# Four output stores of a layered cross network sent as nine row-strided transfers each, with a load moved ahead of them

## The chip, the cores and the metric

The kernel runs on one core of a Trainium2 chip. The metric is the device time of one execution in microseconds; before the change it is 1279.35 us as the median of three runs (1278.41 to 1281.69 us).

## The reference, cut to what matters

The input `x0` has 16384 rows of 4096 float32 numbers. Six layers follow one another, each with one weight vector `w_l` and one bias vector `b_l`:

```python
def step(x, wb):
    wi, bi = wb
    xw = jnp.matmul(x, wi)        # one number for each row
    x_new = x0 * xw + bi + x
    return (x_new, None)
x, _ = jax.lax.scan(step, inputs, (w, b))
```

Each row of the result is therefore that row of `x0` times one number, plus a vector that is the same for all rows. The kernel has to read 256 MiB and to write 256 MiB, and does little else to each number.

## The kernel before, in words

The rows are cut into 128 tiles of 128 rows. A tile is 128 partitions by 4096 float32, 2 MiB, and a row of it is 16 KB that lie together in memory. Ten tiles fit on the chip at once: `tiles` has 5 places for pairs (`N_SLOTS`), with 2 tiles in each (`TB`).

A tile goes through this: SyncE (SP) issues its load. VectorE (DVE) transposes it in two pieces into `blocks` (L261), TensorE (PE) multiplies these with the weights of all layers into `dots` (L405 in the loop over pairs, L363 for the first 2 and the last 24 tiles, which are done one by one), ScalarE (ACT) spreads the sums (L219), a few small steps on PE, ACT and DVE turn them into the one number of each row (`scale`), and DVE writes the result over the tile (L285, two halves of 2048 columns) and raises `tiles_done`. SP then issues the store.

All large transfers go through SP's queue, in an order that the code writes out by hand. In iteration `n` SP waits until tile `n` is done, issues its store (L155), then waits until tile `n - 3` has been stored (`LAG` is 3), since the tile to be loaded next goes to the same place, and issues the load of tile `n + 7` (L143). Each place has one semaphore for its landed loads (`x_landed`) and one for its stores (`y_stored`). A transfer raises its semaphore by 16 in all. A wait for a store is therefore a wait for all its shares, whichever of the chip's 16 DMA engines carries them. The last tile is stored in four parts by columns (L168), and the kernel ends when all stores have landed.

In the startup ScalarE issues six small loads through a queue of its own: the 24 strips of `w` (24 partitions of 4 KB), four loads of rows of `b` (6 partitions each, 2 rows of 2 KB on each), and the 24 strips of `b` (24 partitions of 4 KB).

Of the kernel before, what the change touches and what calls it, by code (L numbers as in the profile page):

```python
# [9 lines left out]
P = 128  # L10
Q = 32
G = P // Q
TB = 2
# [5 lines left out]
N_SLOTS = 5  # L19
HEAD, TAIL = 2, 24  # L20
STORE_PARTS = 4
LAG = 3
LAST_PAIR_OF_PREP = N_SLOTS - 1


def cross_network(nc, x, w, b, out):
    rows, D = x.shape
    L = w.shape[0]
    n_tiles = rows // P
# [13 lines left out]
    out_pairs = out.rearrange("(q t p) d -> q p t d", p=P, t=TB)  # L43
# [4 lines left out]
    with ExitStack() as ctx:  # L48
        def sb(name, shape):
            return ctx.enter_context(nc.sbuf_tensor(name, shape, F32))  # L50
# [4 lines left out]
        def sem(name):  # L55
            return ctx.enter_context(nc.semaphore(name))

        tiles = sb("tiles", [P, N_SLOTS, TB, D])
# [29 lines left out]
        y_stored = [[sem(f"y_stored{s}_{t}") for t in range(TB)] for s in range(N_SLOTS)]  # L88
# [41 lines left out]
        def place_of(n):  # L130
            return n // TB, n // TB % N_SLOTS, n % TB

        def weights_of(g):
            rows = slice(g * Q, (g + 1) * Q)
            into = weights[rows, :, g * LP:g * LP + L].rearrange("p (j k) l -> p j l k", j=G)
            turned_rows = w_turned[rows, :].rearrange("p (k q) -> p k q", q=Q)
            return into, turned_rows[:, :, 0:STRIPS].rearrange("p k (l j) -> p j l k", j=G)

        @block.sync
        def _(sp):  # L140
            def load(n):
                q, s, t = place_of(n)
                sp.dma_start(tiles[:, s, t, :], x_pairs[q, :, t, :]).then_inc(x_landed[s][t], 16)  # L143

            for n in range(TB * LAST_PAIR_OF_PREP):
                load(n)
            load(TB * LAST_PAIR_OF_PREP + 1)
            sp.wait_ge(weights_ready, G)
            sp.wait_ge(bias_summed, 2)
            sp.wait_ge(strips_summed, 1)  # L150
            load(TB * LAST_PAIR_OF_PREP)
            def store(n):
                q, s, t = place_of(n)
                sp.wait_ge(tiles_done, n + 1)
                sp.dma_start(out_pairs[q, :, t, :], tiles[:, s, t, :]).then_inc(y_stored[s][t], 16)  # L155

            for n in range(n_tiles - 1):
                store(n)
                into = n - LAG + TB * N_SLOTS
                if TB * N_SLOTS <= into < n_tiles:  # L160
                    q, s, t = place_of(into)
                    sp.wait_ge(y_stored[s][t], 16 * (q // N_SLOTS))
                    load(into)
            q, s, t = place_of(n_tiles - 1)
            for i in range(STORE_PARTS):
                at = slice(i * D // STORE_PARTS, (i + 1) * D // STORE_PARTS)
                sp.wait_ge(tiles_done, n_tiles + i)
                sp.dma_start(out_pairs[q, :, t, at], tiles[:, s, t, at]).then_inc(y_stored[s][t], 16)  # L168
            for n in range(n_tiles - TB * N_SLOTS, n_tiles):
                q, s, t = place_of(n)  # L170
                last_stores = 1 if n < n_tiles - 1 else STORE_PARTS
                sp.wait_ge(y_stored[s][t], 16 * (q // N_SLOTS + last_stores))

        @block.gpsimd
        def _(pool):
# [23 lines left out]
        def _(act):  # L199
# [7 lines left out]
            for g in range(G // 2, G):  # L207
                place = weights_of(g)
                nc.scalar.copy(place[0], place[1]).then_inc(weights_ready, 1)  # L209
# [31 lines left out]
        def _(dve):  # L241
# [53 lines left out]
            for g in range(G // 2):  # L295
                place = weights_of(g)
                nc.vector.tensor_copy(place[0], place[1]).then_inc(weights_ready, 1)
# [142 lines left out]
```

## Time and profile before

| | |
|---|---|
| median of three runs | 1279.35 us |
| the profiled execution, its own time | 1279.0 us |
| its span in the profile | 1277.3 us |
| VectorE busy | 91% of the span |
| DMA, queue of SP | 98.7% of 16 engines' span |
| TensorE busy | 62% |

The span is the time from the first to the last instruction of the profiled execution, and 1.7 us of that execution's own time lie around it. The share of a DMA queue is the time that its packets took, divided by 16 times the span: 98.7% means that nearly all of the 16 engines carried something nearly all the time. A packet is a row of a transfer, or the write of 4 bytes with which an engine tells a semaphore that its share has landed. The profile counts such writes among the packets under 512 B.

### The profile page before, as it was taken

To read this page: it belongs to the slowest core of one execution; us is meant where nothing else is said; L and a number is where in the kernel's file an instruction comes from. 1 tells how busy PE (TensorE), PEld (TensorE's weight loads), DVE (VectorE), ACT (ScalarE), POOL (GpSimd) and SP (SyncE) were. 2 spreads that over 40 slices of the span, in tenths; PEclk is the share of its full clock that TensorE was granted. 3 is DMA by queue.
4 is the path that set the end of the run, shared out by engine and by line. 5 is a ranking of instruction groups with operands and counts; after the bars stand their busy time and mean duration, and the time that the engine had idled before them with its cause. 6 is when DMAs were issued, how large, how long until landed. Compare 5 with 4: busy or idle time off the path is not lost.

```text
span 1277.3 us, 22775 instructions
## 1 busy us (share of the span) xinstructions
PE 790.4 (62%) x10394; PEld 739.8 (58%) x10394; DVE 1167.0 (91%) x652; ACT 109.5 (9%) x390; POOL 4.3 (0%) x17
## 2 busy tenths in 40 slices
PE   7677666666556556656566556565666457676661
PEld 3666656656456556556566556565565457675561
DVE  5999999998898988989989889899999999999893
ACT  2000000000000000000000000000000011111110
POOL 1000000000000000000000000000000000000000
PEclk9777787777877877877777787777777877778766
DMA  9999999999999999999999999999999999999994
GB/s 369 427 399 432 430 431 432 431 431 430 432 430 433 428 433 429 432 429 432 431 432 430 431 430 431 432 431 431 431 431 430 431 428 429 428 427 428 427 412 172
DMA packets 37480, 537.74 MB, mean 421 GB/s; under 512 B 4192, under 2 KB 4192, under 8 KB 4800
## 3 DMA queue, kind: packets, MB, share of 16 engines
q1 hardware_dynamic: 37296, 536.89, 98.7%
q8 instruction: 28, 0.46, 0.1%
q10 hardware_dynamic: 144, 0.30, 0.1%
q14 instruction: 12, 0.10, 0.0%
HBM read 268.73 MB, written 268.44 MB: 421 GB/s over the span
## 4 chain that ended last, share of the span: by engine, by line
DMA 58%; DVE 33%; issue 4%; PE 2%; SPq 1%; ACTq 0%; ACT 0%; DVEq 0%
DMA tiles<-in_r_inputs_dram 48%; DVE tiles L285 17%; DVE blocks L261 16%; DMA out_dram<-tiles 9%; DMA tiles<-in_L_rec_b_dram 1%; PE dots L363 1%; SPq L155 1%; DVE scale L273 0%; PE strips L353 0%; PE dots L405 0%; ACTq L202 0%; PE scratch L343 0%; ACT spread L219 0%; PE turned L374 0%; DVEq L48 0%
## 5 line engine op out<-in xcount | busy, mean ns | idle before, releaser
L405 PE MATMUL dots<-blocks,weights 128*64 128x128 f32 x6528 | 554.7, 349 | 308.6 <-DVE blocks L261 308.5
L405 PEld LDWEIGHTS dots<-blocks,weights 128*64 128x64 f32 x6528 | 526.6, 185 | 329.0 <-DVE blocks L261 328.8
L261 DVE STREAM_TRANSPOSE blocks<-tiles 128x2048 f32<-128x2048 f32 x256 | 576.1, 2288 | 76.5 <-issue 65.5
L285 DVE SCALAR_TENSOR_TENSOR tiles<-tiles,scale,c_low 128x2048 f32<-128x2048 f32 x129 | 299.1, 2319 | 0.9
L285 DVE SCALAR_TENSOR_TENSOR tiles<-tiles,scale,scratch 128x2048 f32<-128x2048 f32 x129 | 299.8, 2325 | 0.0
L363 PE MATMUL dots<-blocks,weights 128*64 128x64 f32 x3328 | 148.8, 273 | 52.4 <-DVE blocks L261 45.3
L363 PEld LDWEIGHTS dots<-blocks,weights 128*64 128x64 f32 x3328 | 144.9, 187 | 56.6 <-issue 56.4
L219 ACT ACTIVATE spread<-dots,group_mask 128x128 f32<-128x128 f32 (+1 forms) x308 | 82.3, 350 | 1038.8 <-PE dots L405 849.9
L374 PE MATMUL turned<-layer_sel,spread 128*128 128x8 f32 x512 | 71.0, 262 | 93.1 <-ACT spread L219 93.1
L374 PEld LDWEIGHTS turned<-layer_sel,spread 128*128 128x128 f32 x512 | 64.3, 194 | 109.3 <-issue 80.4
L229 ACT ACTIVATE growth<-turned,ones 128x16 f32<-128x16 f32 (+1 forms) x77 | 20.9, 271 | 81.9 <-PE turned L374 81.9
L273 DVE TENSOR_TENSOR_SCAN scale<-growth,cw 128x6 f32<-128x6 f32 x128 | 13.7, 139 | 0.4 <-ACT growth L229 0.4
L343 PE MATMUL scratch<-tiles,ones 6*128 6x512 f32 x16 | 9.1, 877 | 0.5 <-DMA tiles<-in_L_rec_b_dram 0.5
L336 PE MATMUL strips<-tiles,copies 24*128 24x512 f32 x4 | 3.7, 1089 | 6.3 <-DMA tiles<-in_L_rec_w_dram 6.3
L292 DVE STREAM_TRANSPOSE tiles<-strips 128x1024 f32<-128x1024 f32 x1 | 1.2, 1249 | 6.5 <-PE strips L336 6.5
L343 PEld LDWEIGHTS scratch<-tiles,ones 6*128 6x128 f32 x16 | 2.5, 245 | 6.1 <-DMA tiles<-in_L_rec_b_dram 4.9
L336 PEld LDWEIGHTS strips<-tiles,copies 24*128 24x128 f32 x4 | 1.2, 318 | 7.3 <-issue 7.3
L303 DVE CUSTOM_DVE_ANT_0 tiles<-strips,tiles 24x1024 f32<-24x1024 f32 x1 | 1.2, 1212 | 3.9 <-PE strips L353 3.9
L353 PE MATMUL strips<-tiles,earlier 24*24 24x512 f32 x4 | 3.6, 1053 | 0.0
L209 ACT COPY weights<-tiles 32x768 f32<-32x768 f32 x2 | 3.0, 1513 | 4.9 <-DVE tiles L292 4.9
L211 ACT COPY c_low<-scratch 128x2048 f32<-128x2048 f32 x1 | 1.9, 1865 | 3.8 <-PE scratch L343 3.8
L353 PEld LDWEIGHTS strips<-tiles,earlier 24*24 24x24 f32 x4 | 0.5, 138 | 2.9 <-DMA tiles<-in_L_rec_b_dram 1.5
(24 smaller groups left out, 11.6 us busy)
## 6 DMA issues: line engine op xcount, KB each, us to landing
tiles<-in_r_inputs_dram SPq DMA_DIRECT2D x128, 2048.0 KB, 30.3
out_dram<-tiles SPq DMA_DIRECT2D x127, 2048.0 KB, 25.9
out_dram<-tiles SPq DMA_DIRECT2D x4, 512.0 KB, 7.0
tiles<-in_L_rec_w_dram ACTq DMA_DIRECT2D x1, 96.0 KB
tiles<-in_L_rec_b_dram ACTq DMA_DIRECT2D x4, 24.0 KB
tiles<-in_L_rec_b_dram ACTq DMA_DIRECT2D x1, 96.0 KB
```

The lines of the kernel that those rows point to most:

```text
L155: sp.dma_start(out_pairs[q, :, t, :], tiles[:, s, t, :]).then_inc(y_stored[s][t], 16)
L219: nc.scalar.activation(spread[:, 0:n_of, :, g, :], dots[:, 0:n_of, :, :], ACT.Copy, scale=group_mask[:, g:g + 1]).then_inc(dots_spread, 1)
L229: nc.scalar.activation(growth[:, 0:n_of, :], turned[:, 0:n_of, :], ACT.Identity, bias=ones[:, 0:1]).then_inc(growth_ready, 1)
L261: nc.vector.transpose(blocks[:, p % PLACES, :], source).then_inc(blocks_ready, 1)
L273: nc.vector.tensor_tensor_scan(scale[:, u % 2, t, 0:L], growth[:, t, 0:L], cw[:, 0:L], 1.0, ALU.mult, ALU.add).then_inc(scale_ready, 1)
L285: done = nc.vector.scalar_tensor_tensor(out=tile[:, at], in0=tile[:, at], scalar=scale[:, u % 2, t, L - 1:L], in1=c, op0=ALU.mult, op1=ALU ...
L336: nc.tensor.matmul(strips[:, k, :], copies[0:STRIPS, :, :], strips_w[:, k * BANK:(k + 1) * BANK], start=True, stop=True).then_inc(w_copied, 1)
L343: last = nc.tensor.matmul(scratch[:, j, :], ones[j * Q:j * Q + L, :], b_rows[j * Q:j * Q + L, h, :], start=True, stop=True, tile_position= ...
L353: nc.tensor.matmul(strips[0:STRIPS, k, :], earlier[0:STRIPS, 0:STRIPS], strips_b[:, k * BANK:(k + 1) * BANK], start=True, stop=True).then_ ...
L363: last = nc.tensor.matmul(dots[at:at + KM * Q, 0, :, :], weights[:, h * PIECE // Q + k:h * PIECE // Q + k + KM, :], blocks[:, p % PLACES, ...
L374: last = nc.tensor.matmul(turned[:, t, :], spread[:, t, m, :, :], layer_sel[:, m, :], start=(m == 0), stop=(m == KM - 1))
L405: last = nc.tensor.matmul(dots[at:at + KM * Q, :, :, :], weights[:, c * CH // Q + k:c * CH // Q + k + KM, :], place[:, :, k * Q:(k + KM) * Q],
```

## The change

The stores of tiles 30, 60, 90 and 120 are no longer one transfer of 128 rows. Each is nine transfers: the one numbered `r` takes rows `r`, `r + 9`, `r + 18` and so on. The first two have 15 rows and the other seven have 14, which makes 128. Every one of them raises the semaphore of its place by 16, so that the store as a whole raises it by 144, and `stored_by(n)` computes what the semaphore shows when tile `n` and all before it in its place are stored. In the four iterations of these tiles the wait and the load of tile `n + 7` are issued first, and the nine stores after it; in all other iterations the order is what it was.

```diff
+STEP = 9
+IN_NINE = (30, 60, 90, 120)
@@
+        def stored_by(n):
+            return sum(16 * STEP if m in IN_NINE else 16 for m in range(n % (TB * N_SLOTS), n + 1, TB * N_SLOTS))
@@
             def store(n):
                 q, s, t = place_of(n)
                 sp.wait_ge(tiles_done, n + 1)
-                sp.dma_start(out_pairs[q, :, t, :], tiles[:, s, t, :]).then_inc(y_stored[s][t], 16)
+                if n in IN_NINE:
+                    for r in range(STEP):
+                        sp.dma_start(out_pairs[q, r:P:STEP, t, :],
+                                     tiles[r:P:STEP, s, t, :]).then_inc(y_stored[s][t], 16)
+                else:
+                    sp.dma_start(out_pairs[q, :, t, :], tiles[:, s, t, :]).then_inc(y_stored[s][t], 16)
 
             for n in range(n_tiles - 1):
-                store(n)
+                if n not in IN_NINE:
+                    store(n)
                 into = n - LAG + TB * N_SLOTS
                 if TB * N_SLOTS <= into < n_tiles:
                     q, s, t = place_of(into)
-                    sp.wait_ge(y_stored[s][t], 16 * (q // N_SLOTS))
+                    sp.wait_ge(y_stored[s][t], stored_by(into - TB * N_SLOTS))
                     load(into)
+                if n in IN_NINE:
+                    store(n)
```

On SP around tile 30, before. The rows are SP's queue in order; in `y_stored3_1` the first number is the place of the pair and the second the tile in it. Row 57 is the store of tile 30, row 58 the load of tile 37.

```order
56 L143 DMA tiles<-in_r_inputs_dram 128x4096 [waits y_stored3_0]
57 L155 DMA out_0_dram<-tiles 128x4096 [waits tiles_done]
58 L143 DMA tiles<-in_r_inputs_dram 128x4096 [waits y_stored3_1]
59 L155 DMA out_0_dram<-tiles 128x4096 [waits tiles_done]
60 L143 DMA tiles<-in_r_inputs_dram 128x4096 [waits y_stored4_0]
```

The same place in the changed kernel, where the lines 143 and 155 have become 148 and 165:

```order
56 L148 DMA tiles<-in_r_inputs_dram 128x4096 [waits y_stored3_0]
57 L148 DMA tiles<-in_r_inputs_dram 128x4096 [waits y_stored3_1]
58 L162 DMA out_0_dram<-tiles 15x4096 [waits tiles_done]
59 L162 DMA out_0_dram<-tiles 15x4096
60 L162 DMA out_0_dram<-tiles 14x4096 x7
61 L165 DMA out_0_dram<-tiles 128x4096 [waits tiles_done]
62 L148 DMA tiles<-in_r_inputs_dram 128x4096 [waits y_stored4_0]
```

The load of tile 37 has moved ahead of the store of tile 30, and that store has become nine rows of the queue.

On SP at the last load, before. Row 237 is the store of tile 120, row 238 the load of tile 127, which is the last load of all; rows 239 and 240 are the stores of tiles 121 to 126 and the four parts of tile 127.

```order
236 L143 DMA tiles<-in_r_inputs_dram 128x4096 [waits y_stored3_0]
237 L155 DMA out_0_dram<-tiles 128x4096 [waits tiles_done]
238 L143 DMA tiles<-in_r_inputs_dram 128x4096 [waits y_stored3_1]
239 L155 DMA out_0_dram<-tiles 128x4096 [waits tiles_done] x6
240 L168 DMA out_0_dram<-tiles 128x1024 [waits tiles_done] x4
```

And in the changed kernel:

```order
242 L148 DMA tiles<-in_r_inputs_dram 128x4096 [waits y_stored3_0]
243 L148 DMA tiles<-in_r_inputs_dram 128x4096 [waits y_stored3_1]
244 L162 DMA out_0_dram<-tiles 15x4096 [waits tiles_done]
245 L162 DMA out_0_dram<-tiles 15x4096
246 L162 DMA out_0_dram<-tiles 14x4096 x7
247 L165 DMA out_0_dram<-tiles 128x4096 [waits tiles_done] x6
```

Here the store of tile 120 has moved behind the wait for tile 117 (`y_stored3_1`) and the last load. The other engines' instructions are the same in both kernels.

## Rows read from the trace of the kernel before

**Rows 1.** The page: the span, and each engine's busy time.

```profile
span 1277.3 us, 22775 instructions
## 1 busy us (share of the span) xinstructions
PE 790.4 (62%) x10394; PEld 739.8 (58%) x10394; DVE 1167.0 (91%) x652; ACT 109.5 (9%) x390; POOL 4.3 (0%) x17
```

**Rows 2.** DMA view of 100:1000 and of 1000:1240: packets and MB; issues, us to landing.

```profile
q1 hardware_dynamic: 26620, 387.66, 100.7%
...
out_dram<-tiles SPq DMA_DIRECT2D x93, 2048.0 KB, 25.3
...
out_dram<-tiles SPq DMA_DIRECT2D x25, 2048.0 KB, 39.2
```

**Rows 3.** Whose end SP waited for: 300:600, 1000:1100 and 1100:1200 (us, times, longest).

```profile
SPq L155 <- DVE tiles L285: 267.7, 30, 10.6
...
SPq L143 <- DMA out_dram<-tiles: 37.5, 7, 8.5
...
SPq L143 <- DMA out_dram<-tiles: 91.9, 10, 9.5
```

**Rows 4.** Busy time by stretch at the end; the last columns are DMA share, GB/s.

```profile
1256.00:1262.00 6.00, 0.00 (x0) 0.00 (x0) 0.69 (x1) 0.00 (x0) 0.00 (x0) 0.50 0.96 386
1262.00:1264.00 2.00, 0.00 (x0) 0.00 (x0) 0.00 (x0) 0.00 (x0) 0.00 (x0) 0.50 0.13 53
1264.00:1276.00 12.00, 0.00 (x0) 0.00 (x0) 0.00 (x0) 0.00 (x0) 0.00 (x0) 0.50 0.06 27
```

**Rows 5.** DMA view of the stretch 1264:1276: all packets, by size.

```profile
DMA packets 47, 0.32 MB, mean 27 GB/s; under 512 B 5, under 2 KB 5, under 8 KB 35
```

**Rows 6.** The page's DMA queues; q10 is ScalarE's, q1 is SP's.

```profile
q1 hardware_dynamic: 37296, 536.89, 98.7%
...
q10 hardware_dynamic: 144, 0.30, 0.1%
```

**Rows 7.** DMA view, stretches 7.55:7.95 and 7.95:8.45, end of the first load.

```profile
DMA packets 15, 0.17 MB, mean 415 GB/s; under 512 B 4, under 2 KB 4, under 8 KB 5
...
DMA packets 18, 0.16 MB, mean 328 GB/s; under 512 B 5, under 2 KB 5, under 8 KB 9
...
q1 hardware_dynamic: 9, 0.15, 74.6%
q10 hardware_dynamic: 9, 0.02, 8.5%
```

**Rows 8.** DMA view, last load before the stores: 53.00:53.36, 53.36:54.05, 54.88:55.05, 55.05:55.70.

```profile
DMA packets 16, 0.20 MB, mean 546 GB/s; under 512 B 4, under 2 KB 4, under 8 KB 4
...
DMA packets 16, 0.26 MB, mean 380 GB/s; under 512 B 0, under 2 KB 0, under 8 KB 0
...
DMA packets 10, 0.10 MB, mean 578 GB/s; under 512 B 4, under 2 KB 4, under 8 KB 4
...
DMA packets 16, 0.26 MB, mean 403 GB/s; under 512 B 0, under 2 KB 0, under 8 KB 0
```

**Rows 9.** DMA view, third store, 14.59 later: 67.59:67.95, 67.95:68.66, 69.47:69.64, 69.64:70.29.

```profile
DMA packets 11, 0.11 MB, mean 319 GB/s; under 512 B 4, under 2 KB 4, under 8 KB 4
...
DMA packets 13, 0.21 MB, mean 300 GB/s; under 512 B 0, under 2 KB 0, under 8 KB 0
...
DMA packets 8, 0.08 MB, mean 482 GB/s; under 512 B 3, under 2 KB 3, under 8 KB 3
...
DMA packets 17, 0.26 MB, mean 403 GB/s; under 512 B 1, under 2 KB 1, under 8 KB 1
```

**Rows 10.** SP's stores in 300:600: duration ns min/median/max.

```profile
L155 SPq DMA_DIRECT2D out_dram<-tiles x30: 332/332/337, 308.5 to 596.2; - x30
```

**Rows 11.** SP in order of time, from the store of tile 120 on (start, us).

```profile
1197.77 0.46 SPq L155 DMA_DIRECT2D out_dram<-tiles  x1
1207.29 0.34 SPq L143 DMA_DIRECT2D tiles<-in_r_inputs_dram  x1
```

More of the change, by code:

```diff
@@ L170, in _ @@
                 q, s, t = place_of(n)
-                last_stores = 1 if n < n_tiles - 1 else STORE_PARTS
-                sp.wait_ge(y_stored[s][t], 16 * (q // N_SLOTS + last_stores))
+                more = 0 if n < n_tiles - 1 else STORE_PARTS - 1
+                sp.wait_ge(y_stored[s][t], stored_by(n) + 16 * more)
         @block.gpsimd
```

## The prediction, made before the changed kernel was run

> **What bounds the kernel now.** I read the page first. The span is 1277.3 us and VectorE is busy for 91% of it [rows 1], but the queue of SP fills 98.7% of the time of 16 DMA engines [rows 6], so the transfers bound the kernel and VectorE has some 9% to spare. Next comes the end of the span, by stretches: until 1262 us nearly all DMA engines are busy (share 0.96), from 1264 to 1276 us the share is 0.06 and the rate 27 GB/s [rows 4]. One sixteenth is 0.0625. So in the last 12 to 14 us a single DMA engine works and everything else is done: one engine, called the laggard here, sets the end. Third, the waits of SP: from 300 to 600 us it waits for VectorE alone, 267.7 of 300 us, but from 1000 us on its loads wait for stores that have not landed, 37.5 us in one stretch of 100 us and 91.9 us in the next [rows 3], and a store takes 39.2 us to land in place of 25.3 [rows 2]. A store has landed when the last engine has carried its share. The laggard falls behind all through the run, and somewhere past 1000 us it begins to pace SP, and through it all others.
>
> Its speed follows from the rows. In 900 us 387.66 MB went through 16 engines [rows 2], 26.9 GB/s each, so a row of 16384 B takes 0.609 us, and a share of 8 rows 4.87 us. The laggard at the end has the same rate, 27 GB/s [rows 4]. Since it always has work queued, what is added to its work anywhere is added to the end, one for one, and what is added to the other 15 only is hidden by the 12 us and more that they are ahead.
>
> **How a transfer is shared out.** The question is how many of the 128 rows the laggard gets in the new form. The page shows the rule. SP's queue has 37296 packets [rows 6]: 259 transfers of 128 rows and 16 semaphore writes are 259 x 144 = 37296. ScalarE's six small loads have 144 packets [rows 6]. Their rows are 24 + 24 + 4 x 12 = 96, so 48 are semaphore writes: fewer than 6 x 16, and just what 12 + 12 + 4 x 6 gives. A load of 24 partitions goes to 12 engines and one of 6 partitions to 6, the largest number up to 16 that divides the partitions. By that, a transfer of 15 rows goes to 15 engines and one of 14 rows to 14, one row each. In the nine transfers together 14 engines get 9 rows, the fifteenth 2, and the sixteenth none, where each got 8.
>
> The Trainium skill, page "DMA: Bandwidth & Descriptors", section "Why a DMA increments its semaphore by 16 and not by 1", states the same rule and adds that these are always the lowest-numbered engines; the counts of packets agree with the rule, and the numbering isn't in the rows.
>
> **Is the laggard one of the two that are relieved?** The packets have no engine in the views, but their times do. When the first load ends, four semaphore writes come between 7.55 and 7.95 us, and up to 8.45 us SP's queue moves only whole rows (9 packets of 0.15 MB) [rows 7]: these four are the engines that carry none of ScalarE's packets, the 16 minus the 12. They are as far ahead at the last load before the first store: 4 writes in 53.00:53.36, none in the next 0.69 us, and four of the other twelve together at 54.88:55.05, with none in the 0.65 us behind these [rows 8]. Three stores later, at the same offsets, the four leaders still come within 0.36 us, with nothing behind them for 0.71 us, but of the four later ones only 3 are left in their slot and one comes in the 0.65 us behind it [rows 9]. So it is the stores that are slow on one engine, by 0.06 to 0.3 us each in this stretch, and that engine is one of the twelve, not of the four. If the sets nest (12 inside 14 inside 15), the relieved two are among the four leaders, and the laggard gets 9 rows. That it is the same engine all along I take from there being one.
>
> **The change part by part.**
> - Rows: the laggard carries one more in each of four stores: 4 x 0.609 = 2.4 us, all of it on the path.
> - Semaphore writes: 9 in place of 1, so 32 more. In the 12 us at the end there are 47 packets of 0.32 MB, 5 of them semaphore writes, 30 quarter rows and 12 rows [rows 5]: 12 x 0.609 + 30 x 0.152 = 11.87 us, which leaves 0.13 us for 5, or at most 0.026 us each. The bounds are 0 and 32 x 0.026 = 0.8 us; I take 0.2, since part of the 0.13 us is the edge of the stretch. It is also the nearest row to a write's waiting for its data to land, and shows none.
> - Issuing: nine stores at 0.332 us [rows 10] are 3.0 us on SP, against 0.33. In 300:600 SP has 267.7 us of waiting in 30 iterations [rows 3], 8.9 us each, which covers the 2.7 us more. Fifteen rows could take SP longer to issue than 128; up to 1 us each would be covered. What stands behind them is the next store, whose queue in the engines is 25 us deep [rows 2]. Cost 0.
> - The load ahead of the store: through tile 90 the wait of that load costs SP nothing now (no such wait in 300:600 [rows 3]), so the load goes out some us earlier, and the store behind it. At tile 120 it is otherwise: the store went out at 1197.77 us and the load of 127 only at 1207.29 us, after the wait for store 117 [rows 11]. Now store 120 stands behind that wait, and is 9.9 us late. The laggard, which has just ended store 117, still has loads 124 to 126 and stores 118 and 119 queued, 5 x 4.87 = 24 us, so it doesn't run dry; the others may, for 4.9 us, within what they are ahead. Cost 0, if that cover were gone at most 9.9 us. Its work after the last load stays as it is, 6 stores and 4 parts against some 15 us of computing.
> - Row access: nobody in this kernel reads a row of another engine's partitions in a steady stretch. In the new form engine e reads partitions 9e to 9e+8. A gain from that is excluded, as the rate is already an engine's steady one; a loss is bounded by a second reader's halving every one of the laggard's 36 rows, 36 x 0.609 = 22 us. I take 0, since no row shows such a toll: the only transfers that crossed are ScalarE's small loads, and 9 of their packets beside 9 of SP's in 0.5 us [rows 7] are too short a meeting to show one or to exclude it. Both ends stay for the range.
>
> Sum: 2.4 + 0.2 = 2.6 us, 0.2% more. The span becomes 1279.9 us, and with the 1.7 us around it 1281.6. The profiled execution (1279.0) lies 0.35 us below the median, so I say 1282.0.
>
> **The rivals.**
> *The laggard is relieved.* If it is the sixteenth engine it loses 4 x 8 rows, 19.5 us, and ends at 1258; then the other 15 set the end, at 1262 us [rows 4] plus 2.6, or a little less, since they are no longer held up behind it: a span near 1263 and a time of 1265. For it speaks nothing but that 19.5 us would cover the 14 us by which the laggard ends late [rows 4]; against it the leaders of [rows 7 to 9]. The Trainium skill, "DMA: Bandwidth & Descriptors", section "Latency and other measured facts", says that engines 7 and 15 are usually slower, which it ties to another way of issuing. By that, with 15 as the laggard, this rival holds, and with 7 the forecast. I give it 0.10.
>
> *Rows that cross cost.* Two engines reading partitions behind one path into the memory would each go at half speed. The laggard trails the others by up to some 14 us (39.2 us to landing against 25.3 [rows 2]), so it reads its nine rows while they do other transfers, half of which are stores: half of 36 rows doubled is 11 us, 1293 in all. The point from which it decides is two crossed rows in each nine (4.9 us in total), which leads past 1286. For it: the laggard at the end, alone, is no faster than with all others at work, 27 against 26.9 GB/s [rows 2, 4], so the limit is a path of its own, which may be the one into the memory. Against it: the nine rows of an engine spread over its neighbours, and a crossing lasts a row or two at most. The Trainium skill, "SBUF — State Buffer", section "Door 1: The DMA port swizzle", says that 16 ports serve eight partitions each at 27.2 GB/s and that a transfer goes no faster than the ports it reaches; by that the rival holds. No row here shows two engines at one port for long. Chance 0.27.
>
> *A smaller toll on each of the 36 small transfers,* on SP or in the engines, of 0.04 to 0.15 us on the laggard (36 x 0.15 = 5.4 us): 1284 to 1288. Chance 0.13. The wait that moves ahead at tile 120 is the largest piece of it.
>
> **How the numbers follow.** The forecast has 0.50: 1282.0, itself 1280.5 to 1283.5. About 0.3% or 3.8 us is what a measurement of this kernel can tell from no change, so it counts as the same. Faster 0.10 is the first rival; slower 0.41 is the other two and the upper edge of the forecast; the same 0.49. The range leaves out the first rival and the far end of the second: 1279 to 1296.
>
> **What would show it.** In the profile after, SP's queue has 36 transfers for 4: with 4 x (2 x 15 + 7 x 14) = 512 semaphore writes in place of 64 its packets rise from 37296 to 37744. If the split is another, the sum is void. The end again has a stretch of 12 us or more at a share of 0.06 and 27 GB/s. If the share falls from 0.9 to 0 at once and the span is near 1263, the laggard was relieved. If rows cross at a cost, the stretch after a nine-fold store shows packets of 16 KB that take more than 0.62 us, a rate below 431 GB/s, and SP waits for stores from an earlier time than 1000 us. Stores in nine that take SP over 1 us each, or the laggard idle after 1207 us, would make it the third rival.

## The result, and the profile after

The changed kernel takes 1295.99 us (median of four runs, 1290.43 to 1298.49) against 1280.5 us for the kernel before beside it: ratio 1.0123, 95% interval 1.0107 to 1.0139. It is 15.5 us slower. Of the kernel with six cut stores, below, two of six executions count as slow (1.5% or more above its fastest), and its ratio leaves them out. The forecast was 1282.0 us; the time is near that of the second rival (1293), at the far edge of the range. The profiled execution took 1297.8 us, a span of 1296.1 us against 1277.3 [rows 1].

The page of the changed kernel first: the span, one row of the busy times, the rate in 40 slices, SP's queue (packets, MB, share of 16 engines), and the small stores by size.

```profile
span 1296.1 us, 22807 instructions
...
PE 789.2 (61%) x10394; PEld 738.8 (57%) x10394; DVE 1166.9 (90%) x652; ACT 109.8 (8%) x390; POOL 4.3 (0%) x17
...
GB/s 372 426 403 429 429 432 431 430 433 430 402 429 431 431 430 431 431 430 432 416 421 425 430 430 431 430 428 428 400 416 408 400 421 426 429 427 430 405 373 159
...
q1 hardware_dynamic: 37744, 536.89, 98.3%
...
out_dram<-tiles SPq DMA_DIRECT2D x28, 224.0 KB
...
out_dram<-tiles SPq DMA_DIRECT2D x8, 240.0 KB
```

VectorE does the same work (1166.9 against 1167.0 us). The queue has exactly the 37744 packets of the forecast, so the split is as worked out. What changed is the rate: slices of 32 us that hold a nine-fold store fall to 402, 416 and 400 GB/s, and from about 900 to 1040 us the whole stretch is low (400 to 416).

Next the end, busy time by stretch as in [rows 4] (the last columns are the DMA share and GB/s):

```profile
1272.00:1278.00 6.00, 0.00 (x0) 0.00 (x0) 1.58 (x2) 0.00 (x0) 0.00 (x0) 0.50 0.95 385
1278.00:1280.00 2.00, 0.00 (x0) 0.00 (x0) 0.00 (x0) 0.00 (x0) 0.00 (x0) 0.50 0.49 197
1280.00:1282.00 2.00, 0.00 (x0) 0.00 (x0) 0.00 (x0) 0.00 (x0) 0.00 (x0) 0.50 0.06 25
1282.00:1295.00 13.00, 0.00 (x0) 0.00 (x0) 0.00 (x0) 0.00 (x0) 0.00 (x0) 0.50 0.06 26
```

One engine alone still works for the last 15 us, at 26 GB/s. The laggard was not relieved, and everybody else ends 17 us later too (1279 against 1262 us).

Then SP: its instructions in order of time around tile 30 and at tile 120 (start, length):

```profile
309.07 6.48 SPq L148 DMA_DIRECT2D tiles<-in_r_inputs_dram  x2
319.52 7.95 SPq L162 DMA_DIRECT2D out_dram<-tiles  x9
328.43 0.35 SPq L165 DMA_DIRECT2D out_dram<-tiles  x1
...
1212.11 10.28 SPq L148 DMA_DIRECT2D tiles<-in_r_inputs_dram  x2
1222.44 8.96 SPq L162 DMA_DIRECT2D out_dram<-tiles  x9
```

and whom it waits for (us in total, times, longest) in 300:600 and in 900:1000:

```profile
SPq L165 <- DVE tiles L298: 259.4, 30, 13.8
SPq L148 <- DMA out_dram<-tiles: 11.3, 4, 5.7
...
SPq L148 <- DMA out_dram<-tiles: 14.3, 4, 5.6
```

The nine stores take SP 0.9 to 1.0 us each, not 0.33 [rows 10], and its waits for VectorE cover that. The 6.48 us of the two loads at 309.07 are mostly a wait: the second of them goes out only at 315.21 us, when the store of tile 27 has landed. The loads now wait for stores behind each nine-fold store, where before they did so only past 1000 us [rows 3]. Between these places, from 400 to 600 and from 700 to 900 us, there is no such wait. Most of it comes with the order: the kernel in which only the loads are moved ahead (below), with no small transfer in it, has 6.9 us of such waits in 300:600, against 11.3 here, and is no slower than before. So this wait doesn't tell that rows cross at a cost, although the prediction had taken it for a sign of that.

Last, the DMA view of two stretches, 325:375 (store 30) and 900:1070, first in the changed kernel, then in the kernel before:

```profile
DMA packets 1525, 20.60 MB, mean 412 GB/s; under 512 B 267, under 2 KB 267, under 8 KB 267
...
DMA packets 4895, 69.68 MB, mean 410 GB/s; under 512 B 641, under 2 KB 641, under 8 KB 641
```

```profile
DMA packets 1484, 21.60 MB, mean 432 GB/s; under 512 B 165, under 2 KB 165, under 8 KB 165
...
DMA packets 5022, 73.10 MB, mean 430 GB/s; under 512 B 559, under 2 KB 559, under 8 KB 559
```

The engines are busy (share above 0.9) and still move less: rows take longer. In the nine-fold store of tile 60 the nine rows that I take for the laggard's, each starting where the last ended, took 0.66, 0.67, 0.63, 0.70, 1.01, 1.22, 1.25, 1.39 and 1.23 us. Twice 0.61 is 1.22.

### The profile page after: what moved, and what is told of

It reads as the page before. It is cut to its first block, busy times and chain, and to the rows that moved or that the text cites. A ratio compares the mean times of both kernels' runs of the same rounds, so it can differ in the third digit from the quotient of the medians.

```text
span 1296.1 us, 22807 instructions
## 1 busy us (share of the span) xinstructions
PE 789.2 (61%) x10394; PEld 738.8 (57%) x10394; DVE 1166.9 (90%) x652; ACT 109.8 (8%) x390; POOL 4.3 (0%) x17
## 3 DMA queue, kind: packets, MB, share of 16 engines
q1 hardware_dynamic: 37744, 536.89, 98.3%
## 4 chain that ended last, share of the span: by engine, by line
DMA 61%; DVE 31%; issue 4%; PE 2%; SPq 1%; ACTq 0%; ACT 0%; DVEq 0%
DMA tiles<-in_r_inputs_dram 46%; DVE tiles L298 16%; DVE blocks L274 15%; DMA out_dram<-tiles 14%; DMA tiles<-in_L_rec_b_dram 1%; PE dots L376 1%; SPq L165 0%; DVE scale L286 0%; PE dots L418 0%; PE strips L366 0%; ACTq L215 0%; PE scratch L356 0%; ACT spread L232 0%; PE turned L387 0%; DVEq L50 0%
```

## The experiments

Each is an edit of one of the two kernels. The theories that the expectations name are these. A: rows that another engine than usual reads cost (the second rival). B: a toll on each small transfer (the third rival). C: the new order costs. D: the toll is on the side of the output memory.

Differences in us are the ratio's, times 1280. (For the changed kernel that is 15.7, and the 15.5 us used here are the difference of the two medians.) Some readings use a number that no row of a view shows, worked out from the landing times in the traces: for each load, when the last of 16 engines had landed its share (the laggard), and when the ninth had (the bulk), each less the same in the kernel before. It stands in this table, in us; the first figure is the laggard's delay, the second the bulk's. With both traces laid over one another at the start of their spans the figures differ by up to 0.6 us, so they are good to about that.

| load of tile | changed | every eighth | 16 neighbours | nine blocks | tile 60 alone | 5 rows apart | 4 rows apart |
|---|---|---|---|---|---|---|---|
| 38 | 3.5 / 2.3 | 2.0 / 3.8 | 3.7 / 5.7 | 5.1 / 5.8 | -0.5 / -0.1 | -0.2 / 1.6 | -1.2 / -0.6 |
| 62 | 2.8 / 2.2 | 1.3 / 3.5 | 0.1 / 5.4 | 2.2 / 5.8 | -0.2 / 0.2 | 2.4 / 2.8 | -1.5 / 0.6 |
| 70 | 7.1 / 4.8 | 4.5 / 5.8 | 3.7 / 9.7 | 3.8 / 10.3 | 3.4 / 2.6 | 3.8 / 2.9 | -1.6 / 0.7 |
| 86 | 7.0 / 4.5 | 4.4 / 5.5 | 1.5 / 9.4 | 2.9 / 10.0 | 3.3 / 2.3 | 6.5 / 2.6 | -1.6 / 0.4 |
| 102 | 13.0 / 8.3 | 8.2 / 7.7 | 3.0 / 12.4 | 8.2 / 13.2 | 4.0 / 2.0 | 14.8 / 9.5 | -0.9 / 0.0 |
| 110 | 15.0 / 12.2 | 7.5 / 7.1 | 2.1 / 12.2 | 7.3 / 12.7 | 3.3 / 2.4 | 18.8 / 13.9 | -1.1 / -0.5 |
| 126 | 17.3 / 12.5 | 8.0 / 6.7 | 1.0 / 11.3 | 4.7 / 12.6 | 3.3 / 2.3 | 17.8 / 13.1 | -1.4 / -0.7 |

**First, the order.** The kernel before, with only the loads moved ahead:

```diff
+                if n not in IN_NINE:
+                    store(n)
                 ...
                     load(into)
+                if n in IN_NINE:
+                    store(n)
```

> Only the order is changed: in iterations 30, 60, 90 and 120 the load goes out ahead of the store, which is one transfer of 128 rows as before. Theory A (rows read by other engines than usual cost, the order is free): 1280.5 us, within 2 us of before. Theory B (a toll on each small transfer): the same, no small transfer is in it. Theory C (the late store of tile 120 and the moved loads cost): most of the 15.5 us, above 1290 us.

1280.02 us, ratio 1.0008 (0.9998 to 1.0017): free. The counterpart, the changed kernel with the nine stores back ahead of the load:

> The changed kernel with the order of before: in iterations 30, 60, 90 and 120 the nine transfers of the store come ahead of the load again. Since the order alone cost nothing when the store was one transfer (1280.0 us), theory A has it as the changed kernel, 1290 to 1298 us. If the load that lies ahead is what brings the crossed rows beside other stores, it differs by over 4 us.

1299.2 us, 1.0146 (1.01 to 1.0192), a little above what was expected, with an interval that overlaps the changed kernel's. The order explains none of the 15 us.

**Other ways to cut the four stores.** The loop over `STEP` transfers stays, and only what each takes is another. By columns, 128 rows x 512 columns, eight times:

```diff
-STEP = 9
+STEP = 8
-                        sp.dma_start(out_pairs[q, r:P:STEP, t, :], ...
+                        at = slice(r * D // STEP, (r + 1) * D // STEP)
+                        sp.dma_start(out_pairs[q, :, t, at], tiles[:, s, t, at]).then_inc(y_stored[s][t], 16)
```

> The four stores go out as eight transfers each by columns: 128 rows of 512 columns, so each engine keeps its 8 rows and its partitions, and there are 32 transfers for 4. Theory B (a toll on each small transfer or semaphore write): 32/36 of the 15.5 us, about 1294 us. Theory A (crossed rows): no row is crossed, so no more than the smaller packets cost, 64 packets of 2 KB per engine and store in place of 8 of 16 KB; ScalarE's 2 KB packets took 84 ns where an eighth of 611 ns is 76, so 64 x 8 ns = 0.5 us a store and 2 us in all: 1282.5 us.

1288.91 us, 1.0078 (1.0061 to 1.0095), between the two expectations and due to something else. SP in order of time in this kernel:

```profile
318.97 19.57 SPq L163 DMA_DIRECT2D out_dram<-tiles  x8
```

Eight such stores held SP for 19.57 us, and not evenly: the first five took it 0.34 to 0.49 us each, the last three 8.6, 4.3 and 4.2 us. So it isn't the price of one such transfer, but something that stops SP once several are queued; what, isn't shown. The engines' queues ran short behind it: their busy share falls to 0.72 in 630:640 and to 0.55 in 930:940. As a control without crossing rows it is spoilt.

Every eighth row, and 16 neighbouring rows, eight transfers each, so without an extra row for anybody:

```diff
-STEP = 9
+STEP = 8
```

> The four stores go out as eight transfers of every eighth row, 16 rows each, so that all 16 engines get one row of each and 8 of each store, as before; only which engine reads which partition changes, in all but a few rows. Theory A (crossed rows cost): the 2.4 us of the extra row are gone but the toll stays: 1290 to 1305 us. If the usual share of an engine were eight neighbouring partitions, this split would be the usual one and cost nothing, 1281 us. Theory B (toll per transfer): 1294 us. The Trainium skill, page SBUF - State Buffer, section Door 1: The DMA port swizzle, has the 16 rows of such a transfer reach only 8 ports; by that page alone each of the four stores would take twice its 4.9 us, and the sum would be about 1280.5 + 20 = 1300 us.

```diff
-                        sp.dma_start(out_pairs[q, r:P:STEP, t, :], ...
+                        rows = slice(r * P // STEP, (r + 1) * P // STEP)
+                        sp.dma_start(out_pairs[q, rows, t, :], tiles[rows, s, t, :]).then_inc(y_stored[s][t], 16)
```

> The four stores go out as eight transfers of 16 neighbouring rows, one row for each engine. Number of transfers, packets and semaphore writes are those of the split by every eighth row. Theory A (crossed rows cost, by how many engines read one neighbourhood of partitions at a time): far dearer than the split by every eighth row, 1310 to 1340 us. Theory B (toll per transfer): the same as the other eight-fold splits, 1294 us. The Trainium skill, page SBUF - State Buffer, section Door 1: The DMA port swizzle, has 16 neighbouring partitions reach 4 ports of 27.2 GB/s, 109 GB/s in all; by that page alone a 2 MiB store would take 19.3 us in place of 4.9, and four of them 58 us more.

Every eighth row: 1289.42 us, 1.0088 (1.0066 to 1.0111), just under theory A's range and far under the 1300 worked out from the port table. Neighbours: 1283.74 us, 1.0032 (1.0021 to 1.0044), far under both expectations. The same number of transfers, packets and rows for each engine costs 11.3 us in one form and 4.1 in the other. So a toll on each small transfer (the third rival) explains some 4 us at most (5.6 at the upper end of the interval), and which rows a transfer takes decides the rest. Rows are both what is read from the tile and where it is written, and this comparison changes the two together; the runs with fixed partitions below take them apart. The end of the kernel with neighbours, by stretch:

```profile
1262.00:1264.00 2.00, 0.00 (x0) 0.00 (x0) 0.00 (x0) 0.00 (x0) 0.00 (x0) 0.50 0.95 401
1264.00:1270.00 6.00, 0.00 (x0) 0.00 (x0) 0.00 (x0) 0.00 (x0) 0.00 (x0) 0.50 0.77 324
1270.00:1276.00 6.00, 0.00 (x0) 0.00 (x0) 0.00 (x0) 0.00 (x0) 0.00 (x0) 0.50 0.29 117
1276.00:1279.00 3.00, 0.00 (x0) 0.00 (x0) 0.00 (x0) 0.00 (x0) 0.00 (x0) 0.50 0.05 20
```

Where one engine was alone from 1264 us before [rows 4], now some twelve of sixteen work on to 1270. In the table the bulk is 11 us late and the laggard 1 us. The bulk pays, out of its lead, and between the stores the laggard stops falling behind it (3.7 to 0.1 from tile 38 to 62, while the bulk stays at 5.5; in the kernel before it falls behind by 4.0 us in the same stretch).

Nine transfers of 14 or 15 neighbours, the closest relative of the change:

```diff
-                        sp.dma_start(out_pairs[q, r:P:STEP, t, :], ...
+                        at = 14 * r + min(r, 2)
+                        rows = slice(at, at + (15 if r < 2 else 14))
+                        sp.dma_start(out_pairs[q, rows, t, :], tiles[rows, s, t, :]).then_inc(y_stored[s][t], 16)
```

> The changed kernel, but each of the nine transfers takes 14 or 15 neighbouring rows (0 to 14, 15 to 29, then 14 each) in place of every ninth row. Every engine gets as many rows as in the changed kernel, so the slowest one still gets 36 instead of 32, there are as many transfers and as many packets (37744). Only which engines share a path to the partitions at one time is other. If the crossing of rows costs, and 8 blocks of 16 neighbouring rows cost 4.3 us in all: 1280 + 4.3 + 4 x 0.61 = 1286.7, from 1285 to 1289. If the cost lies in the extra rows and the number of transfers, whatever rows they take: 1296.

1285.36 us, 1.0048 (1.0034 to 1.0062), 6.1 us: as expected. Transfers, their sizes, packets and each engine's number of rows are those of the change. So 9.6 of the 15.5 us lie in which rows each transfer takes, and the extra row, with the ninth small transfer, costs the difference from eight blocks, 2.0 us, for which the prediction had 2.4 (the two intervals leave it some 2 us either way). In 900:1070 this kernel moves

```profile
DMA packets 5006, 71.26 MB, mean 419 GB/s; under 512 B 655, under 2 KB 655, under 8 KB 655
```

The changed form for tile 60 alone (`IN_NINE = (60,)`):

> Only the store of tile 60 goes out as nine transfers. If each of the four costs the same, and nothing else does, a quarter of the changed kernel's 15.5 us: 1279.5 + 3.9 = 1283.4 us. In the trace of the changed kernel the laggard lost 4.3 us at this tile: 1283.8 us.

1282.56 us, 1.0034 (1.0009 to 1.0059): 4.4 us, which agrees with a quarter (3.9), but its interval goes from 1.2 to 7.6 us.

**Which side the toll is on.** In these runs the blocks of 16 neighbouring output rows are kept, and what is read is always the same 16 partitions, so the other rows of these tiles are never stored. First 0 to 15:

```diff
-                        sp.dma_start(out_pairs[q, rows, t, :], tiles[rows, s, t, :]) ...
+                        sp.dma_start(out_pairs[q, rows, t, :], tiles[0:P // STEP, s, t, :]) ...
```

> As the split into blocks of 16 neighbouring rows, but all eight transfers of a split store read the same partitions, 0 to 15, while they write to the same places in the output memory as there. The output rows of tiles 30, 60, 90 and 120 are therefore wrong in all but the first block. Theory A (the toll is at the side of the partitions, engines that read one neighbourhood share its rate): with no way out of each other's way, 16 engines on 4 paths take 4 times 0.611 us for a row, 19.5 us for a store in place of 4.9, and four stores 58 us: about 1338 us, with rows of about 2.4 us. Theory D (the toll is at the side of the output memory): the same as the split by blocks, 1283.7 us. The Trainium skill, page SBUF - State Buffer, section Door 1: The DMA port swizzle, gives these 16 partitions 4 ports, as theory A has it.

1313.25 us, 1.0256 (1.0234 to 1.0279). Nothing but the partitions that are read differs from 16 neighbours, so the toll is on the partitions' side. It is 25 us less than theory A had (1338). The bulk does pay nearly all of it, 14.5 us at the load of tile 38 and 28.5 at that of tile 70, for 14.6 us expected of each store; the laggard is only 10.4 and 19.8 us late there and makes up some of it between the stores. By stretch around the store of tile 30:

```profile
330.00:340.00 10.00, 6.64 (x64) 6.40 (x64) 9.55 (x7) 0.00 (x0) 0.00 (x0) 0.66 1.08 415
340.00:350.00 10.00, 6.43 (x72) 6.11 (x72) 10.00 (x5) 1.41 (x5) 0.00 (x0) 0.83 1.02 123
350.00:360.00 10.00, 4.00 (x66) 3.52 (x67) 10.00 (x8) 0.00 (x0) 0.00 (x0) 0.97 0.89 234
```

and the rate in 325:375 us, in 40 slices, from the DMA view:

```profile
GB/s 433 426 459 419 419 446 433 419 433 446 419 302 170 144 118 131 105 105 105 105 92 131 131 131 223 367 419 380 419 341 393 262 301 393 419 419 433 419 433 433
```

All 16 engines are busy (share 1.02) and move 92 to 131 GB/s together, about a quarter of 431. Of 221 whole rows that began between 336 and 356 us, 83 took 2.2 to 2.6 us, four times 0.61. Then partitions 0, 8, 16 to 120 (`tiles[0:P:STEP, ...]`):

> The same, but the eight transfers all read partitions 0, 8, 16 to 120. The output rows of tiles 30, 60, 90 and 120 are wrong in most places. Theory A with the map of ports of the Trainium skill, page SBUF - State Buffer, section Door 1: The DMA port swizzle (these 16 partitions lie on 8 ports, 2 on each): rows of 1.2 us, a store of 9.8 us in place of 4.9, 20 us in all, about 1299 us. Theory A with eight neighbouring partitions to one path: no more than a meeting here and there, below 1284 us. Theory D (output memory): 1283.7 us, as the split by blocks, since the output side is the same.

1292.1 us, 1.0091 (1.0062 to 1.012), 7 us under theory A's 1299. And 0, 2, 4 to 30 (`tiles[0:32:2, ...]`), which tells two maps of the paths apart:

> As the two runs in which all eight transfers of a split store read the same 16 partitions (the output is wrong in these tiles), now partitions 0, 2, 4 to 30. With 0 to 15 it was 1313 and rows took up to 2.54 us (four times 0.61), with 0, 8 to 120 it was 1292 and rows 1.25 us (twice). If a path serves eight neighbouring partitions, these sixteen lie on four paths, as 0 to 15 would on two: 1313 or so, rows of 2.5 us, 105 to 131 GB/s in the split store. If four neighbours share a path and the next four are on another, as the port table of the Trainium skill has it, 0 to 30 reach eight paths, two engines on each: 1292 (1287 to 1297), rows of 1.25 us, some 220 GB/s.

1295.97 us, 1.0126 (1.0109 to 1.0143). The rate in 325:375 us, first with every eighth partition, then with the even ones:

```profile
GB/s 433 465 419 419 446 433 419 419 459 419 433 420 354 275 249 249 328 341 367 393 354 367 354 288 301 380 406 419 419 446 419 446 419 446 419 446 433 419 419 419
```

```profile
GB/s 433 419 439 419 446 419 419 419 419 419 433 420 367 288 210 249 236 210 315 406 328 341 354 367 354 262 341 406 406 433 433 433 433 419 419 433 446 459 433 433
```

In both the bottom is 210 to 249 GB/s, and the commonest slow row takes 1.15 to 1.3 us (59 rows of 402 that began between 336 and 356 us with the even ones). A path for each eight consecutive partitions is excluded: it would have given an eighth of the rate with 0 to 15, all of it with 0, 8 to 120, and a quarter with the even ones. (With the even ones 8 of the 402 rows took 2.4 us or more, which this reading doesn't explain.) The Trainium skill, "SBUF — State Buffer", section "Door 1: The DMA port swizzle", lists 16 ports (paths, as this text calls them), each with four neighbouring partitions and the four that lie 32 further on, at 27.2 GB/s. By it 0 to 15 reach 4 ports (109 GB/s), 0, 8 to 120 and 0, 2 to 30 each reach 8 (218 GB/s): all three rates agree, within a fifth. These runs also say what the output side adds: every eighth partition read all the time and written in blocks costs 11.6 us, and every eighth row read and written, the split further up, 11.3 us. Both read along 8 paths and differ in where they write, so that costs nothing that the intervals (3 to 4 us either way for each) could tell. Last, the changed kernel with the same every ninth partitions in all nine transfers (0, 9, 18 and so on in the first two, 2, 11, 20 and so on in the others):

> The changed kernel, but the nine transfers of a split store read partitions 0, 9, 18 and so on each time (2, 11, 20 and so on where they have 14 rows), and write where the changed kernel writes. The output rows of tiles 30, 60, 90 and 120 are wrong in most places. The laggard still has 9 rows (2.4 us in four stores). Theory A: engines of one split store stay out of each other's way, and only meet engines that are in another transfer: 2.4 us and a part of the toll, 1283 to 1292 us. Theory D (the toll is at the side of the output memory): as the changed kernel, 1296 us.

1293.83 us, 1.0094 (1.0066 to 1.0123). By the Trainium skill's table these 14 or 15 partitions lie on as many ports, so engines in step would cost nothing. It costs 12 us, of which 2.4 are the extra row, and lies 2 us above theory A's range and as near to theory D's 1296, so this run alone doesn't choose between the two. Engines aren't in step: in the kernel before, the laggard lands its share of a load 5.8 us after the ninth engine at tile 38 and 9.6 us at tile 62, more than a whole share (4.87 us). So it comes to its rows while the others are in other transfers, each on its usual path, and would then share one; that this is what costs is the likely reading, and no view shows it engine by engine.

**Which engine sets the end.** The kernel before with 16 extra transfers of 6, 3, 5 or 4 rows of the input to a spare place in the same memory as the output, so that the first 6, 3, 5 or 4 engines get a row more each and no tile is touched:

```diff
+                if n in EXTRA:
+                    sp.dma_start(spare[EXTRA.index(n), 0:2 * EXTRA_ROWS:2, :],
+                                 x_pairs[0, 0:2 * EXTRA_ROWS:2, 0, :]).then_inc(spare_landed, 16)
```

First with six rows that lie together on both sides (`spare[EXTRA.index(n), :, :]`):

> The kernel before, with 16 more transfers of 6 rows of 16 KB from the input to a spare place in memory, one in every fourth iteration from 40 to 100; nothing else is changed. By the packets each goes to 6 engines, one row each. If the laggard is one of these six (which the startup's packets showed), its 16 more rows of 0.61 us are all added: 1279.0 + 9.8 = 1288.8 us. If it isn't, they are hidden by the 12 us and more that the others are ahead: 1279 us. As a check of the packets: SP's queue then has 16 x 12 = 192 more, 37488.

1284.5 us, 1.0035 (1.002 to 1.005), and its premise failed, as the queue shows:

```profile
q1 hardware_dynamic: 37808, 538.46, 98.6%
```

37808 - 37296 is 512, 32 packets for each extra transfer: 96 KB in one piece were spread over all 16 engines, 6 KB for each. With the rows apart the packets are as many as rows say, 37488 - 37296 = 16 x 12:

> The kernel before, with 16 more transfers of 6 rows of 16 KB, whose rows don't lie side by side: rows 0, 2, 4 to 10 of the input go to every second row of a spare place in memory, one transfer in every fourth iteration from 40 to 100. If each goes to 6 engines, SP's queue has 16 x 12 = 192 packets more, 37488. If the laggard is one of these six, its 16 more rows of 0.61 us all reach the end: 1279.5 + 9.8 = 1289.3 us. If it is one of the other ten, they are hidden: 1279.5 us.

1297.33 us, 1.0129 (1.0098 to 1.016).

> The same with 3 rows in each of the 16 transfers: 16 x 6 = 96 packets more. Together with the transfers of 6 rows it tells in which half of the six the laggard is: 1289.3 us if it is one of the first three engines, 1279.5 us if it is one of the other three.

1278.43 us, 0.9988 (0.9979 to 0.9998).

> The kernel before with 16 extra transfers from one place of the output-side memory to another, each of rows 0, 2, 4, 6, 8 of a block (5 rows, so the first five engines get one each). Three rows cost nothing (0.9988) and six cost 17 us (1.0129). If the slowest engine is the fourth or the fifth: 1289 at the least (16 x 0.61 = 9.8 us more), and some 1296 if five cost as six did. If it is the sixth: 1279 to 1281, and then a transfer of five rows relieves it.

1303.01 us, 1.0192 (1.017 to 1.0214).

> As the run with rows 0, 2, 4, 6, 8, but of 4 rows (0, 2, 4, 6) in each of the 16 extra transfers. Three cost nothing (0.9988), five cost 23.5 us (1.0192). If the slowest engine is the fifth: 1278 to 1281. If it is the fourth: 1290 at the least, and some 1300 if four cost as five did.

1278.94 us, 1.0004 (0.9994 to 1.0014). Rows for the first four engines are free, and for the fifth they cost: it sets the end. But 16 rows are 9.8 us, and five cost 24.6 us, six 16.5. The table shows where the excess came: up to the load of tile 86, behind 10 of the 16 rows, the laggard's delay grew from -0.2 to 6.5 us, 0.67 us for each row, and the bulk's to 2.6 us. From there to tile 110 six more rows come, 3.7 us, and the laggard loses 12.3 us and the bulk 11.3. The DMA view of 900:1070, first with five rows, then with four:

```profile
DMA packets 4790, 69.48 MB, mean 409 GB/s; under 512 B 548, under 2 KB 548, under 8 KB 548
```

```profile
DMA packets 5034, 73.08 MB, mean 430 GB/s; under 512 B 572, under 2 KB 572, under 8 KB 572
```

With five rows it has the same low rate as the changed kernel (410), though all its stores are whole. Rows take longer in it: of the whole rows that began in 900:1070, 113 took over 1.1 us, against 2 with four rows. The extra transfers themselves aren't the reason: they run from about 400 us on, and up to 840 us at most 9 rows in each 50 us took over 0.65 us, but 77 to 135 from 840 to 1040. So part of the price isn't the crossing itself, but what comes when the laggard is further behind than before.

**Can the laggard be relieved?** The kernel before with six stores (tiles 20, 35, 50, 65, 80, 95) cut so that twelve engines get 7 rows and the first four 11; then the same for six loads:

```diff
+                parts = [(4, 116), (0, 4), (116, 120), (120, 124), (124, 128)] if n in SHARED else [(0, P)]
+                for a, b in parts:
+                    sp.dma_start(out_pairs[q, a:b, t, :], tiles[a:b, s, t, :]).then_inc(y_stored[s][t], 16)
```

> The kernel before, with six stores (tiles 20, 35, 50, 65, 80, 95) sent as five transfers: rows 4 to 115 as one (7 rows for each engine) and the other 16 rows as four transfers of 4 neighbouring rows. The first four engines get 11 rows, the other twelve 7, the slowest one (the fifth) among them. It loses 6 x 0.61 = 3.7 us, the four get 11 us more, of the 12 to 14 us that they are ahead. If splits cost nothing by themselves: 1275.8. If the crossing of rows costs the slowest engine about 1 us for each split store, as the eight neighbouring blocks cost 4.3 us for four stores: 1278 to 1282.

1309.22 us (1293.77 to 1327.21), 1.0183 (1.014 to 1.0225).

> The same split for the loads of tiles 20, 35, 50, 65, 80 and 95, the stores left whole. The slowest engine loses 3.7 us again: 1275.8 if writing into other engines' partitions costs it nothing, 1278 to 1282 if it costs as reading them does.

1314.24 us, 1.0294 (1.0254 to 1.0333). Both expectations failed by 15 us and more. The rate of the second kernel over its span:

```profile
GB/s 364 428 403 431 431 393 431 431 431 419 402 431 430 431 379 430 431 431 420 366 424 426 426 407 385 399 415 393 386 384 402 405 406 426 428 426 429 427 424 230
```

It dips to between 366 and 402 after each of the first four cut loads and stays at 384 to 415 from slice 24 to 33. I had priced the four neighbouring rows as the eight blocks. But by the port table of the Trainium skill, with which the runs with fixed partitions agree, each of these groups of four neighbours is one path: four engines at a quarter of the rate for four rows. An estimate from these rows: 6 x 4 x 1.83 = 44 us for these four engines, beside the 11 us of their extra rows, against the 12 to 14 us that they were ahead. That it is they, and not the fifth, that now fall behind is argued and not shown. The landings name no engine: with cut loads two to five engines land their share 10 to 23 us after the first at tiles 68 to 104; with cut stores, in an execution of 1327 us, one does, 22 to 25 us after it at tiles 86 to 102. Loads pay too, and more than stores (37.6 against 23.4 us). No way of cutting the stores or loads here beats the kernel before.

## Why the prediction was wrong, point by point

- **What bounds the kernel** held: one engine sets the end in both kernels, and VectorE's time didn't matter.
- **The split** held to the packet, 37744, and **the laggard not relieved** held: it is the fifth of the engines in the order in which rows are dealt out. The first rival falls. If they are dealt out from the lowest number up, it is neither of the two that the Trainium skill ("DMA: Bandwidth & Descriptors", section "Latency and other measured facts") calls usually slower, 7 and 15.
- **The extra row**, 2.4 us, agrees with the runs: 2.0 us between nine blocks and eight, some 2 us either way. The 0.2 us for semaphore writes are too little for any run here to show.
- **Issuing and the load ahead**, 0, held: the order alone is 1.0008. The stores took SP 0.9 us each, inside the bound of 1 us given as covered.
- **Row access** is the step that failed. The prediction bounded it at 0 and 22 us and said "I take 0, since no row shows such a toll". Rows read on shared paths, with what followed from them, cost about 13 us (15.5 less the extra row). Of these, 9.6 are shown by one comparison (nine blocks against every ninth row), which also changes the order of writing; the runs with fixed partitions say that reading is what costs. The value was taken at an end because no row showed the thing, though [rows 2] and [rows 4] had already said that an engine alone is no faster than with all the others. The second rival worked its price out from rows (half of the laggard's 36 rows doubled, 11 us, 1293) and came within 3 us. The prediction's argument against it, that a crossing lasts a row or two, failed where it can be followed: five of the nine rows of tile 60 took between 1.01 and 1.39 us.
- **"What is added to its work anywhere is added to the end, one for one"** also failed. It held while the laggard was no further behind than before (0.67 us of delay for each 0.61 us row up to tile 86 in the run with five rows), and from tile 86 to 110 the same rows brought 12.3 us for 3.7. In the changed kernel the same stretch brings 8.0 us (7.0 to 15.0), about twice what the stores of tiles 30 (3.5) and 60 (4.3, from 2.8) brought, and the mean rate is 410 against 430 GB/s.
- **That the others' time is hidden** by their lead held in the splits by blocks, and explains what I couldn't forecast: blocks of neighbours delay the bulk by 11 to 13 us at the last loads and the laggard by 1 to 5.

Of 15.5 us, then, as an estimate from the table: some 2 are the extra row, some 3 for each nine-fold store come from rows that shared a path, and the rest, 1 to 3 us, is lost around 900 to 1070 us, where the late laggard slows everybody. The last two can't be separated more sharply, since each feeds the other.

What stays open: why neighbours spare the laggard. By the port table of the Trainium skill, four engines in step would share a path in every block of neighbours, and none in every ninth row, so the table alone orders them the wrong way round; what each engine pays depends on how far it is out of step, which I have not measured engine by engine. Why the laggard's lag, once grown, costs all of them rate in whole transfers, is shown but not explained. And that five rows cost more than six is beyond the intervals, and unexplained.

## What to carry to other kernels

In this kernel, with all DMA engines busy, rows of whole 128-row transfers took 0.61 us (their median before). Every cut by rows that was tried, strided or of neighbours, put engines on each other's paths; where two shared one a row took some 1.2 us, where four did some 2.5 us. Price such a cut by the rows of the engine that ends last, not by bytes or packets, and where a trace doesn't show a cost, take the end of the range that a stated mechanism gives, not zero. An engine that sets the end is not an isolated line: when its lag had grown beyond what it was before, the others lost rate too (409 to 410 in place of 430 GB/s).

## What the runs showed of the hardware beyond that

- One store of 128 whole rows took SP 0.33 us, one of 14 or 15 strided rows 0.77 to 0.98 us. Of eight stores of 128 rows x 512 columns in a row the first five took 0.34 to 0.49 us each and the last three 17.1 us together.
- A transfer of six rows lying together in memory on both sides was cut into 16 pieces of 6 KB on all engines; with gaps between the rows it went to six engines.
- The engine that falls behind has no fixed rate of doing so: with 16 neighbours, when the bulk had been delayed by 5.5 us, its lag (last landing less the first) grew by 0.4 us from tile 38 to 62, where before it grew by 4.0. With nine blocks it didn't grow at all.
